# A graph-and-mixer layer with a routed feed-forward: the softmax exponentials of the second stage move from ScalarE to GpSimd, as powers of e

## The reference

```python
xn = layernorm(x)
# graph part: of all edges the output needs only the first 6250
xt = (xn @ weight).reshape(n, 4, 64)
alpha = softmax(leaky_relu(alpha_l[src] + alpha_r[dst], 0.01), axis=1)   # 4 heads
gnn = sum over heads of alpha[:n] * xt[dst[:n]]                          # repeated 4 times
# mixer: linear attention over all rows, then an MLP with the exact gelu
h = gelu((attention(xn) + xn) @ w1 + b1);  mix = h @ w2 + b2 + xn
x2 = x + gnn + mix
# routed feed-forward, 8 experts, all of them computed for every row
f = layernorm(x2)
w = softmax(f @ Wr + br, axis=-1)                                        # 8 experts
h1 = relu(bn(f @ W1[e] + b1)); h2 = relu(bn(h1 @ W2[e] + b2)); y = h2 @ Wo[e] + bo
out = x2 + sum over e of w[:, e] * y
```

## Time and profile before

| | |
|---|---|
| median of 3 runs | 1128.73 us (1128.67 to 1129.51) |
| the profiled execution | 1127.27 us, its span 1125.4 us |
| PE, matmul | 1099.4 us busy, 98% of the span |
| PE, weight load | 985.2 us, 88% |
| VectorE (DVE) | 772.9 us, 69% |
| ScalarE (ACT) | 716.1 us, 64% |
| GpSimd (POOL) | 245.6 us, 22% |
| chain that ended last | PE 87%, DVE 4%, POOL 2%, ACT 1% |

### The profile page before, as it was taken

How to read it: one execution, slowest core, us unless ns; L and a number is a source line. 1 busy time by engine, 2 the same in 40 slices (tenths; PEclk the granted TensorE clock), 3 DMA queues, 4 the chain that set the end, 5 groups by cost and what they waited for, 6 DMA issues and landing times.

```text
span 1125.4 us, 19517 instructions
## 1 busy us (share of the span) xinstructions
PE 1099.4 (98%) x6676; PEld 985.2 (88%) x6676; DVE 772.9 (69%) x1931; ACT 716.1 (64%) x1223; POOL 245.6 (22%) x267
## 2 busy tenths in 40 slices
PE   7989998999999999999999999999999999999998
PEld 5878898898888889888888898888888888888998
DVE  6867865868577586586675865866758658667564
ACT  3767763775665665666656656656666566666665
POOL 2687764211203012012030120120300301100000
PEclk9999999999999999999999999999999999999999
DMA  5789974110111011011110110111101101100000
GB/s 162 193 202 254 250 181 116 49 38 15 44 38 57 1 44 51 17 32 48 39 53 6 44 53 1 48 48 38 53 5 41 55 1 43 33 20 1 1 20 15
DMA packets 78567, 67.83 MB, mean 60 GB/s; under 512 B 27907, under 2 KB 73845, under 8 KB 78469
## 3 DMA queue, kind: packets, MB, share of 16 engines
q1 hardware_dynamic: 73958, 59.48, 19.3%
q0 software_dynamic: 3968, 6.61, 2.3%
q10 hardware_dynamic: 543, 0.51, 0.2%
HBM read 40.77 MB, written 25.80 MB: 59 GB/s over the span
## 4 chain that ended last, share of the span: by engine, by line
PE 87%; DVE 4%; issue 2%; POOL 2%; DMA 2%; SPq 1%; ACT 1%; another core or an unknown queue 0%; DVEq 0%; ACTq 0%; POOLq 0%
PE bank L271 27%; PE bank L273 27%; PE bank L272 27%; DMA weight_stage<-in_L_ffn_W 1%; PE bank L1044 1%; PE bank L1032 1%; PE bank L888 1%; PE bank L1042 1%; POOL gathered L569 1%; DMA accumulated<-in_L_mix_w_qkv 1%; PE bank L1060 1%; PE bank L835 0%; DVE xT_low L1108 0%; DVE sum_squares L1215 0%; POOL ffn_w_low L576 0%
## 5 line engine op out<-in xcount | busy, mean ns | idle before, releaser
L1257 DVE SCALAR_TENSOR_TENSOR accumulated<-bank,router_w,accumulated 128x256 f32<-128x256 f32 (+2 forms) x392 | 170.3, 479 | 200.0 <-PE bank L273 190.1
L613 ACT ACTIVATE h<-weight_stage 128x512 fp32r<-128x512 f32 (+2 forms) x206 | 113.6, 599 | 204.2 <-PE bank L273 183.1
L273 PE MATMUL bank<-ffn_w_high,h 128*128 128x256 f32 (+2 forms) x778 | 220.0, 283 | 0.0
L272 PE MATMUL bank<-ffn_w_low,h 128*128 128x256 f32 (+2 forms) x778 | 219.9, 283 | 0.0
L271 PE MATMUL bank<-ffn_w_high,h 128*128 128x256 f32 (+2 forms) x778 | 219.7, 282 | 0.0
L739 ACT ACTIVATE activated<-bank,bn_cols 128x512 f32<-128x512 f32 (+2 forms) x208 | 156.7, 753 | 56.2 <-PE bank L273 51.0
L739 ACT ACTIVATE weight_stage<-bank,bn_cols 128x512 f32<-128x512 f32 (+2 forms) x208 | 155.4, 750 | 53.9 <-PE bank L273 53.7
L1108 DVE TENSOR_TENSOR h_low<-activated,h_high 128x512 fp32r<-128x512 f32 (+2 forms) x209 | 135.0, 657 | 78.3 <-ACT h_high L613 77.0
L584 POOL DMA_INDIRECT gathered<-node_table,indices x49 | 63.9, 1304 | 533.9 <-DVE residual L1314 519.4
L271 PE MATMUL bank<-xT_high,ffn_w_high 128*128 128x512 f32 (+2 forms) x416 | 159.6, 384 | 0.4 <-DVE xT_low L1108 0.4
L271 PE MATMUL bank<-h_high,ffn_w_high 128*128 128x512 f32 (+2 forms) x416 | 157.8, 379 | 1.5 <-DVE h_low L1108 1.5
(11 more groups left out here) (204 smaller groups left out, 1885.1 us busy)
## 6 DMA issues: line engine op xcount, KB each, us to landing
x_rows<-in_x SPq DMA_DIRECT2D x18, 512.0 KB, 5.3
x_turned<-xT_high SPq DMA_DIRECT2D x22, 256.0 KB, 4.8
x_turned<-xT_low SPq DMA_DIRECT2D x22, 256.0 KB, 6.5
mix_xT_high<-x_turned SPq DMA_DIRECT2D x11, 512.0 KB
mix_xT_low<-x_turned SPq DMA_DIRECT2D x11, 512.0 KB
out<-accumulated SPq DMA_DIRECT2D x11, 512.0 KB, 3.3
weight_stage<-in_L_ffn_W SPq DMA_DIRECT2D x16, 256.0 KB, 5.0
node_table<-gathered SPq DMA_DIRECT2D x22, 130.0 KB, 4.6
```

Source lines behind the costliest of these rows:

```text
L272: nc.tensor.matmul(dst, ah, bl, start=False, stop=False)
L273: last = nc.tensor.matmul(dst, al, bh, start=False, stop=(k == n - 1))
L613: return nc.scalar.activation(dst, src, ACT.Copy)
L1257: last = V.scalar_tensor_tensor(a, Yb[b][0:tp, (t % 2) * D:(t % 2 + 1) * D], wts(ch)[0:tp, t, e:e + 1], a, ALU.mult, ALU.add)
```

## The change

Both exponentials go to GpSimd and are made by its power operation, e to the logit, with a column that holds e as the base, broadcast to the shape of the logits. The warm-up becomes a gelu. The semaphores `s_gexp` and `s_fex` that VectorE waits for now come from GpSimd.

```diff
+        euler = sb("euler", [P, 1])
...
+            nc.gpsimd.memset(euler[:, :], math.e).then_inc(s["euler"], 1)
...
+            def power_of_e(a):
+                return nc.gpsimd.tensor_tensor(a, euler[0:a.shape[0], :].unsqueeze(1).broadcast_to(list(a.shape)), a, ALU.pow)
+
+            def gnn_exp(ch):
+                need(pool, s["glog"], ch.c + 1)
+                power_of_e(ga[0:ch.tp, 0:ch.nt, :]).then_inc(s["gexp"], 1)
+
+            def router_exp(ch):
+                need(pool, s["flg"], ch.c + 1)
+                power_of_e(rl[0:ch.tp, 0:ch.nt, :]).then_inc(s["fex"], 1)
+
+            pool.wait_ge(s["euler"], 1)
             gather(CHUNKS[0], range(CHUNKS[0].nt))
             for ch in CHUNKS:
+                gnn_exp(ch)
                 if not ch.last:
                     if ch.c == 0:
                         pool.wait_ge(s["m_sum"], 1)
...
                     gather(ch.next(), range(0, 2))
                 norm2(ch)
+                if ch.c == 0:
+                    router_exp(ch)
                 if not ch.last:
                     need(pool, s["gmsg"], ch.c + 1)
                     gather(ch.next(), range(2, ch.next().nt))
+                if ch.c > 0:
+                    router_exp(ch)
...
-            nc.scalar.activation(warm[:, :], epsc[:, 0:1], ACT.Exp)
+            nc.scalar.activation(warm[:, :], epsc[:, 0:1], ACT.Gelu)
...
-            def gnn_exp(ch):
-                need(act, s["glog"], ch.c + 1)
-                a = ga[0:ch.tp, 0:ch.nt, :]
-                nc.scalar.activation(a, a, ACT.Exp).then_inc(s["gexp"], 1)
-
...
-            def router_exp(ch):
-                need(act, s["flg"], ch.c + 1)
-                a = rl[0:ch.tp, 0:ch.nt, :]
-                nc.scalar.activation(a, a, ACT.Exp).then_inc(s["fex"], 1)
-
...
-            FRONT = {1: gnn_exp, 2: gelu, 5: x2_high, 6: router_exp}
-            for step in (gnn_exp, gelu, x2_high):
+            FRONT = {2: gelu, 5: x2_high}
+            for step in (gelu, x2_high):
                 step(CHUNKS[0])
             relu1(CHUNKS[0], 0)
-            router_exp(CHUNKS[0])
```

More of the change, by code:

```diff
@@ L3 @@
 from contextlib import ExitStack
+import math
 fp32 = mybir.dt.float32
@@ L201, in build @@
         L1b, L2b, Yb, Fb = bank[0:2], bank[2:4], bank[4:6], bank[6:8]
-        names = """ld_b ld_w0 ld_w1 ld_g ld_bn ld_w1m ld_small id ones eps set_pool w_sum bias_row kv_w kv_mean kv_w2 kv_hi kv_lo
+        names = """ld_b ld_w0 ld_w1 ld_g ld_bn ld_w1m ld_small id ones eps euler set_pool w_sum bias_row kv_w kv_mean kv_w2 kv_hi kv_lo
             g_mean g_w g_prod g_sum g_hi g_lo
```

## The result

The kernel became slower by less than half a per cent: a median of 1133.3 us (8 runs, 1131.54 to 1134.39) against 1128.7 us (8 runs, 1125.48 to 1129.65) for the kernel before, a ratio of 1.0045 with an interval of 1.0034 to 1.0056. The profiled execution took 1133.72 us, its span is 1131.9 us, against 1127.27 and 1125.4 us before.

A forecast was written before the change was run, and what follows sets the result against it. Matmuls bound the steady chunks; only the second stage's start hangs on small VectorE, ScalarE and GpSimd steps. Costs 0.1 + 2.2 + 1.0 = 3.3 us gave 1130.6 profiled, 1132.0 us as the median; range 1129.4 to 1137.0.

The forecast's parts named there:

- The price of a power: GpSimd's power of n elements per partition costs 0.73 + 0.115(n - 2) us: 1.4 for 8, 2.3 for 16, 4.2 for 32.
- The netting of the hold: Overlap with VectorE subtractions (0.19 and 0.64 us) taken off two four-element GpSimd powers, leaving 0.90 us each, 0.085 an element.
- Item 1: First graph exponential, 8 elements: back 1.2 us late, mostly absorbed by VectorE's 1.14 us idle before the gelu; cost 0.1 us.
- Item 2: First router exponential, 16 elements: VectorE stands still behind it, cost 2.2 us; PE's router-transpose wait grows from 0.6 to 2.8.
- Rival (a): PE's clock falls to half after the 2.8 us wait at the router's transpose, adding 1.3 us: 1133.3 us; chance 25%.
- Item 3: Second half of chunk 1's gathers, moved behind the first router exponential: 0.6 us to spare before VectorE's logits, cost 0.
- Item 4: Graph exponential of chunk 1, 16 elements: 1.97 us of cover against 3.0 needed, cost 1.0 us before messages.
- Items 5 and 6: Chunk 1's router exponential, at most 0.4 us late, put at 0; steady chunks' exponentials hidden, cost 0.
- the cover: Time VectorE has other work while steady chunks' exponentials run: router 8.07 us for 5.7 needed, graph 5.2 for 3.8.
- the threshold: Steady chunks' router exponential: with 1.4 us of hold, its 8.07 us are used up when 32 elements cost 6.6 us.
- The table loads: ScalarE's removed loads, 33.4 us: hidden by matmuls in steady chunks, no PE wait behind one, so they shorten nothing.
- rival (d): One table load lay on the path at the start and comes off: faster, 1127.4 us; chance 5%.

The follow-up runs named there:

- e3: Changed kernel with the four exponentials of chunks 0 and 1 back on ScalarE, chunks 2 to 12 on GpSimd; ratio to the kernel before 0.9998.
- e6: The kernel before, unchanged, profiled a second time; second stage 948.3 us.
- e12: Changed kernel with the first gathers of chunk 1 put ahead of chunk 0's graph exponential on GpSimd; ratio to the kernel before 1.0057.
- e1: Changed kernel with 13 filler calls on PE ahead of chunk 0's router transpose; 1130.85 us, ratio to the kernel before 1.0052.
- e2: Changed kernel with only chunk 0's router exponential back on ScalarE; 1126.07 us, ratio to the kernel before 1.0007.
- e4: Changed kernel with every power replaced by an addition on GpSimd, gathers at their new places; ratio to the kernel before 0.9997.
- e5: Changed kernel with fillers in two PE waits, 13 calls before chunk 0's router transpose, 8 before expert 3's second layer; ratio to the kernel before 1.0043.
- e7: The changed kernel, unchanged, profiled and timed a second time; 1130.66 us, ratio to the kernel before 1.0034.
- e11: Kernel before, with GpSimd's first gathers of chunk 1 held until chunk 0's graph logits are made; 1124.24 us, ratio to the kernel before 0.9985.
- e9: Changed kernel with chunk 0's router weights made and turned one step later, at expert 1; ratio to the kernel before 1.0016.
- e8: Changed kernel with a second router power on spare columns in chunks 2 to 12; 1161.27 us, ratio to the kernel before 1.0305.
- e10: As e9, with the last gathers of chunk 1 ahead of chunk 0's router power again; ratio to the kernel before 1.0005.

## Why the prediction was right, and where it was not

The forecast was 1132.0 us, likeliest slower by over 0.2%; it came to 1133.3, inside the range. The mechanism held: the steady chunks pay nothing, and the time is lost at the first exponentials, where VectorE waits. The size is nearer than its steps: one term was too small, a rival came true in part, and a gain was overlooked.

- **The price of a power** was the mis-sized term: 1.4, 2.3 and 4.2 us forecast for 8, 16 and 32 elements, 1.68, 2.89 and 5.45 measured. The netting of the hold misled me. The calls of 16 elements took 2.89 us with no subtraction beside them, 3.02 us in chunk 1, where four run beside them for 1.28 us in all (209.84 to 210.58 and 211.29 to 212.00, the call from 210.01), and 3.28 us in a steady chunk with 1.15 us of them. So a hold is there, as the Trainium skill (GPSIMD Engine Reference, "Key points") says of VectorE instructions with two SBUF inputs, but it was a tenth of the overlap in one call and a third in the other, and not the whole of it as I had taken it to be; the 0.143 us a plain reading of the earlier trace rows gives was the better price.
- **Item 1**, 0.1 us: the gelu split moved from 3.12 to 3.54 us and the router logits by 0.30, so 0.3 to 0.4. The reason I gave failed: the 1.14 us wait "for a release that had nothing to do with the exponential" has to do with the queue that the exponential now stands in. In all four profiles in which GpSimd was issuing the gathers of chunk 1 at that time (before, e3, e6, e12) PE's signal came 1.9 to 3.9 us behind the end of its matmuls (in before the second one; the first is hidden by the table load); in the ten in which these gathers came later (after, e1, e2, e4, e5, e7 to e11) it came within 0.02 us of it. That e11 loses the wait by holding the gathers back, and nothing else, and that e12 gets the late signal by putting them there, shows that their place decides at this hand-over. The change puts an exponential ahead of those gathers and takes this wait away, 1.14 us of VectorE's time in one profile of before, 3.94 in the other.
- **Item 2**, 2.2 us: `weights` begins 3.00 us behind the logits' end, not 0.28, so 2.72, and PE waits 3.1 us and not 2.8. The mechanism stands, and e2 shows it: with this exponential alone put back, the ratio is 1.0007.
- **Rival (a)**, the clock, at 1.3 us, given 25%: it fell at that wait in both profiles of the change, for 2.6 and for 1.4 us. In "after" it fell once more at 220.2 us, and the difference grew by 0.70 us there. Against its use as advice: fillers (e1, e5) kept the clock up at that place and gave nothing that a run can measure, since the signal of L1069 was late then (by 0.5 and 1.3 us) and, in e5, the clock fell elsewhere.
- **Item 3**, 0: right in the change, where `logits` of chunk 1 has no wait in its row and begins 2.2 us behind `add_bias` as before. But the cost was only hidden behind the others: e9 laid 1.97 us of it open. And late signals go with the issuing here too: from L1069's modelled end to its reader 1.57 us in e4, 0.48 in e1 and 1.30 in e5, where the matmul ended while gathers were being issued; 0.03 to 0.05 us in all kernels in which they were over.
- **Item 4**, 1.0 us: 1.16 at `messages`, with a wait of 1.06 us in the row. It lies so close by luck: the call was priced 0.55 us too low (2.34 for 2.89) and the hold 0.41 too high (0.54 for 0.13).
- **Items 5 and 6**, 0: a wait of 0.19 us for the router exponential of chunk 1, which left no mark on the stage; steady chunks 75.60 us. e3 and e8 bear out the cover, and that the threshold lies where 8.07 us put it.
- **The table loads and rival (d)** (5%, one load on the path): in the first profile of before the load ran from 181.43 to 182.71, and VectorE waited for a signal that came after that: nothing, as forecast. In e6 and e3 it stood behind the late signal, and its 1.28 us were in the open once. With the signal on time (e11) VectorE waits 0.19 us behind it. The other loads were worth nothing: e3 keeps 7 of them and e4 2, with ratios of 0.9998 and 0.9997. The switch of 2.66 us with its drain that the Trainium skill gives (ScalarE: Activation LUTs, "What ACT_TABLE_LOAD costs") is not what the rows show here: in that first profile the exponential ended at 181.41, the load ran from 181.43 to 182.71 and the gelu began at 182.72, so a switch took the load's 1283 ns.

By milestones the change costs 0.3 + 2.7 + 1.2 us in waits for powers (4.2, against 3.3 forecast), 1.4 to 3.3 us for the clock, and gives back what before loses at the gelu, 0 to 4 us by its two profiles. The mean of the two profiles of each is 950.8 against 946.3 us: 4.5 us, where the medians say 4.6 and 4.06. That the forecast of 3.3 lies close to it owes something to two omitted terms of opposite sign.

**What stays open.** The place of the gathers decides at the gelu, but gathers in issue do not by themselves make a signal late. In all six profiles in which the last gathers of chunk 1 were issued while PE computed expert 0's first layer (before, e2, e3, e6, e10, e11) its signal reached ScalarE at once. ScalarE's timeline, e6, for a matmul that ended at 194.87 between issues from 191.52 to 196.32:

```profile
194.90 0.55 ACT L739 ACTIVATE activated<-bank,bn_cols 128x240 f32<-128x240 f32 x1 [1.59 <-issue]
```

e9 shows the same: its L1069 ended at 203.73, in the middle of gathers issued from 201.49 to 206.49, and its reader started 0.04 us later. Nor does a late signal come as soon as the issuing ends: in e3 and e6 ScalarE started 1.3 and 1.4 us behind the end of the last issue. In the four profiles with a late gelu the gathers of chunks 0 and 1 formed one row of eight issues, 10.2 us long (170.6 to 180.8 in e6); in the other places named here the rows had four, and the latest signal, of e4's L1069, came 1.57 us late. Whether the number of gathers in a row matters was not tried. The ends of matmuls are modelled, and what holds the signal (the issuing, the transfers behind it, or a path that both use) no run here tells apart. How often executions of before lose 1 us at the gelu and how often 4 was not counted either, with two profiles of it; its times spread over 4.2 us, which would fit.

## What to carry to other kernels

Before small work is moved to an engine with idle time, ask at each place whether somebody stands still behind it: here nobody waited for 22 of the 26 exponentials on GpSimd, and one of 16 elements, at a hand-over where VectorE and PE both waited, made most of the loss. A power on GpSimd costs by the element per partition (0.15 us), so price it from the plain difference of two calls, and take a netted one for a lower bound. And when a wait has no visible releaser ("remote"), look at what GpSimd was issuing at that moment: holding the gathers of the next chunk back by one semaphore gave a ratio of 0.9985 (e11), where taking 21 of the 28 table loads out gave 0.9998 (e3), nothing to be measured.

## What the runs showed of the hardware that was not expected

- At one hand-over PE's completion signals came 1.9 to 3.9 us behind the modelled end of the matmul, in the four of four profiles in which GpSimd was issuing a row of eight indirect gathers (0.94 to 1.23 us each, gaps of 0.30 us), and on time in ten of ten in which the second four came later. At another, in the middle of a row of four, they came on time in six of six.
- GpSimd's `pow` on f32: 1.68, 2.89, 4.16 and 5.45 us for 8, 16, 24 and 32 elements per partition, on 120 to 128 partitions, where an addition of 32 took 0.24 us.
- The granted clock was at half for 6.7 us in one execution and for 3.4 in another of the same program, at the same wait of 3.1 us, which cost 2.6 and 1.4 us.
